# A message-passing layer on one core: when index lists are renewed, and what the gathers wait for

## What is computed

```python
total_edge = concatenate([x[src], x[dst], edge_feats], axis=-1)     # 200000 x 169
nbr_filter = sigmoid(_bn(total_edge @ W1.T + b1, g1, bt1))          # z is total_edge @ W1.T + b1
nbr_core   = softplus(_bn(nbr_filter, g2, bt2))
agg        = segment_sum(nbr_filter * nbr_core, dst, num_segments=12500)
new        = x + _bn(agg, g3, bt3)
return _layernorm(x + new, axis=-1)
```

## Time and profile before

| | |
|---|---|
| median of 3 runs | 2853.16 us |
| the profiled execution's own time | 2841.35 us |
| its span, from the first to the last instruction | 2839.3 us |
| busy: GpSimd (POOL) | 1743.7 us, 61% |
| busy: TensorE matmuls (PE) | 1077.2 us, 38% |
| busy: VectorE (DVE) | 932.8 us, 33% |
| busy: ScalarE (ACT) | 581.7 us, 20% |
| gathers at L386 | 1445.3 us busy, 1532 from p_table, 943 ns each |

### The profile page before, as it was taken

One profiled execution on the slowest core, in us unless ns is written; L12 is line 12 of the kernel. 1 busy time (PEld: TensorE's weight loads), 2 busy tenths in 40 slices (PEclk: granted clock), 3 DMA queues, 4 the chain that ended last, 5 costly groups with the idle time before them and its releaser, 6 DMA issues. The chain is left out here.

```text
span 2839.3 us, 24625 instructions
## 1 busy us (share of the span) xinstructions
PE 1077.2 (38%) x6592; PEld 663.1 (23%) x6592; DVE 932.8 (33%) x1571; ACT 581.7 (20%) x548; POOL 1743.7 (61%) x1678
## 2 busy tenths in 40 slices
PE   4433333333332323233333333333333220377877
PEld 3111111111111111111111111111111110366763
DVE  2211111122121212111112212121212259799895
ACT  0100000000000000000000000000000048899984
POOL 4466666666666666666666666666666640566764
PEclk7655555555555555555555555555555555799898
DMA  5444444444343434344444444365744439687742
GB/s 178 136 119 104 111 115 108 114 101 116 98 121 92 126 95 120 102 112 112 112 112 103 114 100 119 94 175 152 207 127 123 102 93 387 217 278 251 271 129 91
DMA packets 230367, 393.21 MB, mean 138 GB/s; under 512 B 66504, under 2 KB 119302, under 8 KB 217562
## 3 DMA queue, kind: packets, MB, share of 16 engines
q1 hardware_dynamic: 135191, 279.54, 32.0%
q0 software_dynamic: 50048, 51.30, 10.7%
q10 hardware_dynamic: 45067, 61.63, 6.4%
HBM read 297.16 MB, written 95.17 MB: 138 GB/s over the span
## 5 line engine op out<-in xcount | busy, mean ns | idle before, releaser
L386 POOL DMA_INDIRECT rows<-p_table,idx x1532 | 1445.3, 943 | 804.8 <-issue 452.3
L661 DVE TENSOR_TENSOR into_z<-d_in,node_ps 84x1024 f32<-84x1024 f32 x196 | 236.7, 1208 | 951.2 <-DMA d_in<-dst_f 660.2
L436 PE MATMUL xg_ps<-into_z,with_w 128*64 128x512 f32 x384 | 188.2, 1080 | 928.7 <-DVE into_z L661 686.1
L525 ACT ACTIVATE z_sb<-z_ps 128x512 f32<-128x512 f32 x100 | 59.7, 597 | 1806.1 <-remote 1572.6
L436 PE MATMUL z_ps<-into_z,with_w 128*64 128x512 f32 x400 | 174.5, 967 | 374.6 <-issue 327.6
L930 POOL TENSOR_TENSOR h_buf<-h_buf,s_all 128x1536 f32<-128x1536 f32 x66 | 223.5, 3432 | 91.7 <-ACT h_buf L904 91.7
L436 PEld LDWEIGHTS xg_ps<-into_z,with_w 128*64 128x64 f32 x384 | 28.4, 205 | 955.4 <-DVE into_z L661 685.2
L686 DVE BATCH_NORM_STATS2 stats<-z_sb 128x512 f32 (+1 forms) x196 | 135.1, 689 | 353.5 <-issue 233.2
L472 PE MATMUL z_ps<-ident,rows 128*128 128x128 f32 x768 | 186.6, 419 | 162.1 <-DMA rows<-p_table,idx 116.5
L472 PEld LDWEIGHTS z_ps<-ident,rows 128*128 128x128 f32 x768 | 159.6, 308 | 299.7 <-DMA rows<-p_table,idx 165.2
L472 PEld LDWEIGHTS xg_ps<-ident,rows 128*128 128x128 f32 x764 | 167.7, 324 | 178.6 <-issue 151.4
(11 more groups left out here) (136 smaller groups left out, 940.9 us busy)
## 6 DMA issues: line engine op xcount, KB each, us to landing
s_all<-edge_mem SPq DMA_DIRECT2D x110, 768.0 KB, 6.8
d_in<-dst_f SPq DMA_DIRECT2D x97, 672.0 KB
edge_mem<-z_sb ACTq DMA_DIRECT2D x97, 512.0 KB
into_z<-e_main SPq DMA_DIRECT2D x98, 352.0 KB
near<-near_mem SPq DMA_DIRECT2D x65, 504.0 KB, 4.3
near_mem<-near_one SPq DMA_DIRECT2D x97, 336.0 KB
rows<-p_table,idx POOLq DMA_INDIRECT x1532
agg<-edge_mem SPq DMA_DIRECT2D x8, 768.0 KB
```

The costliest lines, as they stand in the source:

```text
L386: gp.indirect_dma_start(out=rows[s][0:size.tile, t, h, :], out_offset=None, in_=table, in_offset=bass.IndirectOffsetOnAxis(ap=idx[s][0:siz ...
L436: mm = pe.matmul(to[h * F:(h + 1) * F, 0:w], which(h)[0:height], into_z[s][0:height, h, 0:w], start=first, stop=False)
L525: act.activation(z_sb[s][:, 0:size.half], z_of(g, s)[:, 0:size.half], ACT.Copy).then_inc(z_copied, 1)
L661: v.tensor_tensor(hot[s][:, :, 0:size.half], d_in[:, s % 2, :, 0:size.half], node_col[0:WIN, bass.ds(g * 2, 2)].rearrange("p (h a) -> p h ...
```

## The change

The renewal of a pair's index list no longer waits for `z_ready` on DVE. It waits until the gathers of both groups that used the list have landed. GpSimd waits for `z_ready` in front of every group, for the z that had used this group's slot, and no longer once for the pair. Each place has one `sem_inc(bumps, 1)`, a counter that nobody waits for.

```diff
@@ gather, on GpSimd
                     if s % 2 == 0:
                         gp.wait_ge(idx_ready, j + 1 + (isinstance(j, int) and j == PAIRS_OF - 1))
-                        after(gp, z_ready, j * 2 - 2)
-                        gp.sem_inc(bumps, 1)
+                    after(gp, z_ready, g - S + 1)
+                    gp.sem_inc(bumps, 1)
                     for t in range(size.tiles):
@@ group, on DVE
                     if s % 2 == 1 and not (isinstance(g, int) and g + S > GROUPS):
-                        v.wait_ge(z_ready, g + 1)
+                        for k in (s - 1, s):
+                            v.wait_ge(gathered[k], (turn + 1) * 2 * TILES * 16)
+                        v.sem_inc(bumps, 1)
                         indices(turn * 2 + s // 2 + 2, s // 2)
```

## The result

The changed kernel takes 2969.9 us, the median of 4 runs (2965.65 to 2991.68), against 2853.26 us for the kernel before on the same chip: a ratio of 1.042 (95% interval 1.040 to 1.045), 117 us slower. The profiled execution took 2974.02 us.

What follows compares the result with a forecast made beforehand. GpSimd's gathers at L386 were taken as the bound, with 47 stalls of 6.5 us from late z signals. A gain of 0.5 and a loss of 0.9 gave 0.30 us times 190 groups, 57 us more: 2910 us, range 2755 to 3000.

Steps and rivals of the forecast that it cites:

- step 1: After GpSimd restarts with group 93, group 94's list copy waits behind the one-hot needing d_in: a new stall of 5.4 us.
- step 2: Groups 94 to 98 then gather unbroken from +16.0 us, their z's and lists being ready in time.
- step 3: z 95, done 24.4 us after the restart, is held until +71.1 us: six groups per cycle, 11.85 us each against 11.55.
- F+0.9: GpSimd's restart with odd group 93, 0.9 us after the moment at which a held z is released.
- fourth rival: A 5.4 us stall is too short to clear the held state; four groups per 51.1 us, 3087 us; chance 8%.
- the first late z held: Upper bound: z 94 is held instead of 4 us late, giving five groups per 61.1 us, 2980 us.
- the shorter hop: Between z and GpSimd's gather, the list copy drops out of the path: 0.26 us less per stall.
- third rival: Lists in time, z still held: four groups per cycle stay, less 47 times 0.26 us, 2841 us; chance 12%.
- second rival: Signals come in time but SyncE stays slow: 11.05 us per group, 2758 us; chance 14%.
- first rival: Signals come through once GpSimd never waits for a copied list; all 47 stalls go, 2546 us; chance 8%.

Runs made afterwards that it cites:

- i1: DVE's part of the change alone (early list renewal, GpSimd waiting for z once per pair), where signals are held: 2829.15 us, 0.993 of the kernel before.
- i3: Changed kernel with the list renewed ahead of the one-hot on DVE, where signals are held: 2828.01 us, 0.992 of the kernel before.
- k2: Changed kernel, but before an odd group GpSimd also waits for the z needed by the next even group: 2840.64 us, 0.995 of the kernel before.
- e6: The changed kernel unaltered, on a chip where no signal was held: 2514.36 us, 0.999 of the kernel before.
- k1: The changed kernel unaltered, run again where signals are held: 2976.02 us, 1.042 of the kernel before.
- i2: GpSimd's part of the change alone (z wait per group, lists renewed when z is finished), where signals are held: 2851.05 us, 1.001 of the kernel before.
- h1: Kernel before, with TensorE giving two of every four groups' signals only after certain gathers have landed: 2864.5 us, ratio 1.009.
- h3: Changed kernel, list renewed ahead of the one-hot, TensorE giving two of every four groups' signals only after certain gathers landed: 2840.2 us, ratio 1.000.
- h4: DVE's part of the change alone, with TensorE giving two of every four groups' signals only after certain gathers landed: 2842.45 us, ratio 1.001.

## Why the prediction was right or wrong

Right was the direction and the shape. GpSimd restarts in front of an odd group; a stall for the list follows one group later, because the copy stands behind the one-hot that waits for d_in (step 1); then five groups run unbroken (step 2); then z is held again (step 3). 31 stalls of either kind were forecast, and 31 and 32 are there. The cycle is six groups, and no engine's work grew.

Wrong was the size: 57 us forecast, 117 measured. **The step that failed is step 1's "a new stall of 5.4 us", with the assumption behind it that GpSimd's restart at F+0.9 lets the next z's and SyncE's steps come at once**, as its restart before the change did. I took the 14.9 us from release to list copy from a cycle in which GpSimd had been dry for 6.5 us and the next z was announced together with the held one. After the change GpSimd needs only one z and restarts on it, after 1.7 to 7.6 us, and in 20 of 31 cycles the rest stays held, with SyncE slow (13.0 us from near_mem to d_in in the cycle shown, 2.2 in the cycle that I read it from). These 20 cycles lose 14.8 us each, 4.6 and 10.2; I had 11.8 (6.4 and 5.4), so they cost 60 us more than forecast. The other 11 behave as step 1 says: 11.6 us, 6.7 and 4.9, in all 2 us less than forecast. With one lone stall of 4 us in front of group 8 that is 62 us, the whole gap between the 366 us that I had for the idle time and the 428 measured.

That a stop can be too short to clear the state was the reason of my fourth rival; but I put it at the even stall of 5.4 us, with z 93 held after it and four groups per cycle, 3087 us. What came is between the two: it is the odd stall that is mostly too short, the z's come out during the second one, and six groups per cycle stay. Of the bounds, the one that I gave for another cause (2980, the first late z held) happens to lie near the result; five groups per cycle, its mechanism, did not occur.

My term for the shorter hop, 0.26 us per stall, is borne out by i1, where it stands alone, if somewhat small: 6.53 to 6.15 us, 0.38 per stall, 18 us over 47, and 21 us measured (the 6.53 is from another chip).

The third rival (lists in time, z still held, four groups per cycle less the hop: 2841, or 0.996) is what i3 and k2 do, at 0.992 and 0.995. The second rival, signals in time with SyncE slow, was seen nowhere.

The first rival, signals that come through whatever the lists do, gave 2546 us. Its number was nearly right for a situation that I had not thought of: on three occasions nothing was held, and then the kernel before takes 2516 us itself. The Trainium skill, SBUF — State Buffer, section Who interferes with whom, says that a DMA never contends with a compute engine and that TensorE and ScalarE wait on nobody. That is said of ports of SBUF. Where nothing is held the trace agrees (0.2 us from TensorE's last matmul to ScalarE's copy); where it is 20.7 us, the matmuls themselves are done and their signal is late, which is no test of that rule; nor does the rule give the first rival's time. What differs between the occasions none of these runs shows.

## What to carry to other kernels

When a wait is made finer so that an engine may go on sooner, ask where it will stop next and what stands behind that place in the other queues: here the stop moved from in front of an even group, where the list was ready, to in front of an odd one, 10 us ahead of a list queued behind a one-hot and its DMA. Put a short renewal that another engine waits for ahead of long work that has its own input to wait for. And where a stall also lets late signals through, a shorter stall isn't cheaper by itself: in 20 of 31 cycles of six groups it took 14.8 us in two pieces, where stops of 6.5 us per four groups (9.8 per six) had done.

Best of what was tried is the changed kernel with the list first, 0.992 (0.991 to 0.994), or with the pairwise wait kept, 0.993 (0.991 to 0.995), where signals are held; both are within 0.2% of the kernel before where they are not.

## What the runs showed of the hardware that I had not expected

- **The same kernel takes 2516 or 2841 to 2857 us.** On three occasions the kernel before took 2515.91 to 2516.49, on four (the first measurement included) 2840.66 to 2856.98, and nothing between, and on each occasion its runs agree within 0.6%. It isn't fixed to a chip: the chip that gave 2516.49 for the kernel before (with e6) gave 2856.98 later (with k1 and k2). The cause is open.
- **Where it is slow, what is late are signals and SyncE's steps, not work.** TensorE's signals are held until GpSimd has paused for some microseconds. Pauses of 1.03 us are not enough; in most stops of 1.7 to 6.3 us one signal gets through and the next don't; behind all 21 odd stops of 6.75 us and more, in two profiles, the next z was copied within 3.2 us. Variants that stop once in four groups (the kernel before, i1, i2, h1, h3, h4) all stop for 6.1 to 7.0 us in the mean, whatever ends the stop.
- **SyncE's slow steps depend on how its program is written.** In the kernel before, 15.3 to 16.6 us from near_mem to d_in in its loop, 6.4 to 6.9 where the same loads are written out; 1.8 to 2.6 in either place where nothing is held (e6, the last pair apart). Other loads join at the same place, so that it is the loop itself isn't shown.
- **A gather's price is by the instruction.** 944 ns for 128 rows and 903 ns for 64, and 0.30 us between two of either kind.
